# Preparing the cross-attention inside the last self-attention group of a decoder layer

## The chip, the cores and the metric

One Trainium2 chip, one core. The metric is the device time of one execution in microseconds (us); the kernel before has a median of 1537.75 us over three runs.

## The reference

One pre-norm decoder layer over x of 8 sequences x 256 tokens x 1024 channels, in float32. Each of its three parts normalises x (mean and variance over the channels) and adds its result to x:

- Self-attention with 32 query and 8 key/value heads of 32 channels. The four projections have weights of sign(w) only and a scale per output channel.
- Cross-attention with 16 heads of 64: `C_q = norm(x) @ Wq_d` (1024 to 128), `C_kv = ctx @ Wkv_d` (1024 to 64), `CqWqk = C_q @ W_qk` (128 to 1024), scores = CqWqk . C_kv / 8 per head, softmax, values = `C_kv @ Wv_u`.
- A gated feed-forward part through rank 256, inner width 2752.

## The kernel before

**Tiling.** The 2048 tokens are worked in four groups of 512 (two sequences, four row tiles of 128). Before a projection each normalised row tile is transposed by PE in two halves (step `turn`, four 128x128 transposes into one bank of PSUM) and evacuated as two parts whose sum is the float32 value (step `split`: ACT writes the high part, L993, DVE subtracts for the low part, L1201). All products with float32 operands are three or two such passes.

**One order for all engines.** A list `ORDER` of steps (`self_order`, L100; `cross_order`, L236; `ffn_order`) is walked by all five engine programs, and each does its share of every step. So the place of a step in the list sets its place in each engine's queue and in SP's queue of DMA issues; an engine that waits in one step does nothing behind it. Two PSUM banks (`proj`) serve all turns and projections in turn; `bank_uses` hands them out in list order.

**Self-attention of a group.** It has 64 head steps (8 key/value heads x 2 sequences x 4 heads). Head i does: `tile` (scores on PE L778, exp on ACT L1017, and on every second head a fold, the sum of two tiles of exps, on POOL L1465), `score` of head i+16 (PE L758, DVE maximum L1270), and, every fourth head, `mix` (values, PE L791) and `sums` (PE L804), after which `sum_turn`, `recip_turn` (DVE) and `finish` (POOL L1483, L1488, L1491, which writes attnT_hi and attnT_lo) normalise a unit of 8 heads. ACT copies the mixed values (L1023) only after POOL's L1483 of the unit before. The exps live in eight `wide` buffers, the folds in four. The rest of each head step is a plan `side[i]`: in groups 0 to 2 the loads, norms and turns of the next group's x (turns at heads 34 to 41) and its first q projections (heads 43 to 63). In the last group the plan is empty from head 34 on. `late` holds the six steps that follow head 63: finish of unit 6; sums and mix; sums; sum_turn; recip_turn; finish of unit 7.

**The seam.** After `late` the last group's output projection runs (`o`, PE L863: 8 tiles x 16 matmuls; DVE L1319 and L1323 add the residual; SP stores x1). `("phase", 2)` then makes ACT, DVE, POOL and SP wait until all self-attention results are made, since the cross-attention's buffers lie over the self-attention's. `cross_order` begins: turns of y (norm of x1) and c (ctx, not normalised) tiles, four each; the raw weights loaded into `x_group` memory (SP L1621 to L1625), high parts made by POOL (L1499 to L1511), low parts by DVE (L1330 to L1343); `lowq` (C_q, PE L877), eight loads of x1 into `x_group` (SP L1630), two `xq` (PE L887; ACT, DVE; eight stack copies by SP L1640), `lowkv` (C_kv, PE L877), loads of group 1's first three row tiles, five `vup` (PE L897), and then the heads of cross-attention: `score` (PE L821, DVE L1298, exps on ACT L1034), flip, evac, values. `attention_order` starts with three scores and then a lead: the norm of y tile 0 of group 1, then v-ups 5 to 7. The first turn of that y tile comes in the first head.

**Row tiles.** Loads go through two rings of row buffers, `xin` (3) and `xres` (2). A load waits on SP until the step that last used its buffer is done (`released`, L607); for a row tile that is the PE transpose of its second half.

## Time and profile before

| | |
|---|---|
| median of three runs | 1537.75 us (1535.91 to 1538.12) |
| the profiled execution | 1539.78 us |
| its span, first to last instruction | 1538.0 us |
| mean granted clock of TensorE | 0.973 |
| PE, DVE, ACT, POOL busy | 91%, 59%, 46%, 34% |
| self-attention heads, groups 0 to 3 | about 77 to 605 us |
| last o projection | 614 to 644.5 us |
| first cross-attention scores | 693.9 us |

An engine's row in the timeline gives the start, the length, the line, what it writes and reads, and in brackets how long the engine stood idle before it and what released it. Lengths of matmuls overlap, since they are pipelined; the distance of two starts is the rate.

### The profile page before, as it was taken

What the parts mean: (1) busy time and instruction counts of PE and PEld (TensorE: products, weight loads), DVE (VectorE), ACT (ScalarE), POOL (GpSimd) and SP (SyncE); (2) the same over time, 40 slices, a digit from 0 to 9 for tenths busy, and PEclk for the clock granted to TensorE, in tenths of its full rate; (3) what the DMA queues carried; (4) which work ended last, traced back from release to release, by engine and by line L of the source; (5) the groups of instructions that cost most, each with busy time, mean ns of one, the idle gap of its engine ahead of it and who ended that gap; (6) DMA issues with size and microseconds to landing.
All of it is one profiled execution on the core that took longest, in us unless ns stands there. A gap on an engine that the chain in (4) does not pass through costs nothing.

```text
span 1538.0 us, 22614 instructions
## 1 busy us (share of the span) xinstructions
PE 1393.0 (91%) x8423; PEld 981.8 (64%) x8423; DVE 908.7 (59%) x1611; ACT 704.8 (46%) x1584; POOL 523.7 (34%) x466
## 2 busy tenths in 40 slices
PE   5888899999999996868989899896999999999998
PEld 3555455555555553447667677675788888887886
DVE  5468555836774563547658486473563663673645
ACT  5165503541452254026747476472553354454452
POOL 2047503851674168112112121031442342342320
PEclk9999899999999998979999999997999999999999
DMA  5776634574537351455536445257210310310111
GB/s 192 104 141 129 118 69 125 92 115 106 108 60 118 105 82 44 147 152 141 164 96 166 137 111 137 70 151 259 76 57 0 110 56 1 110 55 1 69 69 55
DMA packets 94881, 157.55 MB, mean 102 GB/s; under 512 B 9910, under 2 KB 49076, under 8 KB 94772
## 3 DMA queue, kind: packets, MB, share of 16 engines
q1 hardware_dynamic: 94772, 156.11, 41.0%
q8 instruction: 67, 1.10, 0.3%
q14 instruction: 42, 0.34, 0.1%
HBM read 82.15 MB, written 25.17 MB: 70 GB/s over the span
## 4 chain that ended last, share of the span: by engine, by line
PE 66%; DMA 10%; DVE 9%; ACT 5%; issue 4%; SPq 3%; POOL 3%; DVEq 0%; POOLq 0%; ACTq 0%
PE bank L937 15%; PE bank L949 7%; PE bank L863 7%; DMA q_stack<-hi_lo 6%; PE bank L744 5%; PE bank L922 3%; PE bank L698 3%; PE bank L877 3%; PE bank L778 3%; PE bank L758 3%; PE bank L791 2%; PE bank L821 2%; PE bank L848 2%; PE bank L962 2%; DMA xq_stack<-xhi_lo 2%
## 5 line engine op out<-in xcount | busy, mean ns | idle before, releaser
L1465 POOL TENSOR_TENSOR fold<-wide 128x512 f32<-128x512 f32 x128 | 163.2, 1286 | 238.7 <-ACT wide L1017 222.1
L1017 ACT ACTIVATE wide<-bank 128x512 f32<-128x512 f32 x256 | 150.0, 596 | 144.0 <-PE bank L778 141.4
L1270 DVE TENSOR_REDUCE neg_top<-bank 128x2 f32<-128x512 f32 x256 | 170.6, 680 | 61.2 <-PE bank L758 59.7
L1541 POOL TENSOR_TENSOR v_lo<-v_all,v_hi 128x512 fp32r<-128x512 f32 x88 | 122.7, 1396 | 246.5 <-ACT v_hi L1102 246.5
L778 PE MATMUL bank<-q_stack,k_stack 98*128 98x512 f32 x256 | 138.7, 545 | 4.0 <-ACT wide L1017 3.7
L937 PE MATMUL bank<-pT_hi,v_hi 128*128 128x512 f32 x352 | 137.3, 390 | 2.6 <-POOL v_lo L1541 2.6
L937 PE MATMUL bank<-pT_hi,v_lo 128*128 128x512 f32 x352 | 137.2, 390 | 0.0
L937 PE MATMUL bank<-pT_lo,v_hi 128*128 128x512 f32 x352 | 136.9, 389 | 0.0
L1422 DVE SCALAR_TENSOR_TENSOR inner<-bank,b_cols,inner 128x512 f32<-128x512 f32 x88 | 65.9, 749 | 112.6 <-PE bank L937 109.3
L758 PE MATMUL bank<-k_stack,q_stack 96*128 96x256 f32 x512 | 111.6, 305 | 16.1 <-DMA q_stack<-hi_lo 13.9
L1034 ACT ACTIVATE wide<-bank,neg_max 128x256 f32<-128x256 f32 x256 | 120.2, 489 | 10.0 <-DVE neg_max L1298 10.0
L758 PEld LDWEIGHTS bank<-k_stack,q_stack 96*128 96x128 f32 x512 | 93.9, 195 | 43.2 <-DMA q_stack<-hi_lo 19.7
L1125 ACT ACTIVATE inner_hl<-inner 128x512 fp32r<-128x512 f32 x88 | 55.6, 632 | 135.4 <-DVE inner L1422 135.4
L949 PE MATMUL bank<-inner_hl,u_hi 128*128 128x512 f32 x352 | 111.3, 397 | 3.7 <-DVE inner_hl L1425 3.7
L1298 DVE TENSOR_REDUCE neg_max<-bank 128x2 f32<-128x512 f32 x128 | 87.1, 685 | 41.0 <-PE bank L821 40.7
L1518 POOL TENSOR_TENSOR x_group<-x_group,tmp 128x512 f32<-128x512 f32 x32 | 40.9, 1278 | 198.4 <-DVE tmp L1382 198.4
L863 PE MATMUL bank<-signs_o,attnT_hi 128*128 128x512 f16 x256 | 99.2, 387 | 8.6 <-POOL attnT_lo L1491 8.0
L1473 POOL TENSOR_TENSOR bn<-bn,neg_half 128x1 f32<-128x1 f32 x48 | 29.9, 622 | 222.3 <-DVE bn L1195 222.3
L744 PE MATMUL bank<-hT_hi,signs_qkv 128*128 128x512 f16 x256 | 100.3, 392 | 1.5 <-DVE hi_lo L1246 1.5
L1425 DVE TENSOR_TENSOR inner_hl<-inner,inner_hl 128x512 fp32r<-128x512 f32 x88 | 65.0, 738 | 61.5 <-ACT inner_hl L1125 61.5
L698 PE MATMUL bank<-ident,xin 128*128 128x128 f32 x456 | 74.7, 293 | 29.3 <-DVE hT_lo L1201 9.3
L863 PE MATMUL bank<-signs_o,attnT_lo 128*128 128x512 f16 x256 | 98.7, 386 | 0.0
(176 smaller groups left out, 3136.5 us busy)
## 6 DMA issues: line engine op xcount, KB each, us to landing
q_stack<-hi_lo SPq DMA_DIRECT2D x96, 256.0 KB, 5.7
xin<-x_scratch SPq DMA_DIRECT2D x33, 512.0 KB, 4.7
xq_stack<-xhi_lo SPq DMA_DIRECT2D x128, 128.0 KB, 2.4
x_res<-in_x SPq DMA_DIRECT2D x22, 512.0 KB, 4.7
x_scratch<-x_res SPq DMA_DIRECT2D x16, 512.0 KB, 2.8
xin<-in_ctx SPq DMA_DIRECT2D x16, 512.0 KB, 4.6
x_group<-x_scratch SPq DMA_DIRECT2D x32, 256.0 KB, 3.3
x_scratch<-x_group SPq DMA_DIRECT2D x32, 256.0 KB, 2.6
```

The lines of the kernel that those rows point to most:

```text
L698: t = pe.transpose(J[:, i * P:(i + 1) * P], src[:, kb * P:(kb + 1) * P], ident[:, :])
L744: t = pe.matmul(J[:, :], sW[:, kb, tq * P:(tq + 1) * P], hT[p][:, kb, :], start=kb == 0 and p == 0, stop=kb == KB - 1 and p == 1)
L758: t = pe.matmul(tops[n % 2][:, a * SEQ:(a + 1) * SEQ], qst[U % Q_STACKS][0:SUB, r, b * SEQ + a * P:b * SEQ + (a + 1) * P], kst[0:SUB, tq, ...
L778: pe.matmul(tiles[m % 2][:, :], kst[0:SUB + 2, tq, b * SEQ + kt * P:b * SEQ + (kt + 1) * P], qst[U % Q_STACKS][0:SUB + 2, 2 * hp:2 * hp + ...
L863: t = pe.matmul(J[:, :], OT[p][:, tq, m * P:(m + 1) * P], sWo[:, tq, n * GT:(n + 1) * GT], start=tq == 0 and p == 0, stop=tq == KB - 1 and ...
L937: t = pe.matmul(G[:, :], v1s[W % 3][wp][:, s, r, :], pT[g % 2][ap][:, r, :], start=r == 0 and (wp, ap) == (0, 0), stop=r == RB - 1 and wp ...
L949: t = pe.matmul(z_banks[r][:, :], u2s[W % 3][wp][:, r, :], inner_hl[W % 2][:, ap, :], start=f == 0 and (wp, ap) == (0, 0), stop=f == FB - ...
L1017: act.activation(PT[m % PT_RING][:, :], tiles[m % 2][:, :], ACT.Exp).then_inc(sem["tile_exped"], 1)
L1034: t = act.activation(Pb[:, a * SEQ:(a + 1) * SEQ], S[:, a * SEQ:(a + 1) * SEQ], ACT.Exp, bias=mx[:, a:a + 1], accum_out=total)
L1270: dve.tensor_reduce(neg_top[U % 2][:, r, b, :], tops[n % 2][:, :].rearrange("p (a b) -> p a b", a=QT), AX.X, ALU.max, negate=True).then_in ...
L1465: pool.tensor_tensor(fold[f % FOLD_RING][:, :], PT[2 * f % PT_RING][:, :], PT[(2 * f + 1) % PT_RING][:, :], ALU.add).then_inc(sem["folded" ...
L1541: pool.tensor_tensor(lo[:, :, :, 0:n], inner_gu(f, n), hi[:, :, :, 0:n].bitcast(F32), ALU.subtract).then_inc(sem["iw_lo"], 1)
```

## The change

Names: y is the normalised x1, c the context; raw weights are numbered 0 (Wq_d), 1 (Wkv_d), 2 (W_qk), 3 (Wv_u).

- The last group's plan gets the load and split of raw weight 1, loads, turns and splits of all c and y tiles of cross-attention group 0, the four y norms, `lowkv` in eight chunks of three matmuls (heads 46 to 53), and the loads of raw weights 0, 2 and 3 (heads 58, 60, 62).
- Behind head 63, `raw_split` 0, the first half of the first o tile and `lowq` stand between the late steps; `raw_split` 2 and 3 and the first two `xq` stand in the o projection.
- Raw weights land in the row rings, not in `x_group`; their high parts are made by ACT in place of POOL. DVE still makes the low parts.
- Memory is laid out anew: `ckv0`, `actT1` (c) and `wkv_down` over the signs and hT of the q/k/v projections, `actT0` (y) over `hi_lo` and three of four query stacks, `wq_down` over the fourth, `w_qk`, `ckv1` and `wv_up` over the key stack. Waits guard this: c splits and raw_split 1 wait for the last q projection, y splits for all stack copies and the tiles up to head 55, the other raw splits for all tiles, the first evacuation of `lowq` for all sums.
- The o matmuls wait for attnT_lo of four units per half, not for all eight at once.
- `cross_order` starts with the `x_group` loads and the three loads of group 1, then five `vup`.

```diff
-        put(57, ("o_load", g, 1))
+        if g + 1 < NG:
+            put(57, ("o_load", g, 1))
+        else:
+
+            put(7, ("raw_load", 1))
+            for m, at in enumerate((12, 16, 20, 36)):
+                put(at, ("load", "c", 0, m))
+            put(34, ("raw_split", 1))
+            for m, at in enumerate((34, 36, 38, 42)):
+                for h in range(2):
+                    put(at + h, *turn("c", 0, m, h))
+            for m, at in enumerate((38, 40, 44, 45)):
+                put(at, ("load", "y", 0, m))
+                put(at + 6, ("norm", "y", 0, m))
+            for c in range(KB):
+                put(46 + c, ("lowkv", 0, c))
+            put(46 + KB - 1, ("lowkv_out", 0))
+            for m in range(TILES):
+                for h in range(2):
+                    put(56 + 2 * m + h, *turn("y", 0, m, h))
+            for i, at in ((0, 58), (2, 60), (3, 62)):
+                put(at, ("raw_load", i))
...
-            for step in late:
-                order += step
-            for i in range(2 * TILES):
+            order += late[0] + late[1] + [("raw_split", 0), ("o_load", g, 1)] + o_parts(g, 0)[0]
+            order += late[2] + late[3] + late[4] + [("lowq", 0), ("lowq_out", 0), ("raw_split", 2)] + late[5]
+            order += o_parts(g, 0)[1]
+            for i in range(1, 2 * TILES):
                 for part in o_parts(g, i):
                     order += part
                 if i in (1, 3):
                     order.append(("o_load", g, i // 2 + 2))
-                if i < 3:
-                    order.append(("load", "y", 0, i))
-                elif i < 6:
-                    order.append(("norm", "y", 0, i - 3))
+                if i == 2:
+                    order.append(("raw_split", 3))
+                if i in (3, 4):
+                    order += [("xq", 0, i - 3), ("xq_out", 0, i - 3)]
...
-    order = []
-    for i, t in enumerate((0, 1, 2, 4, 5, 3, 6, 7)):
-        order += turn(0, t, 0) + turn(0, t, 1)
-        if i < 5:
-            order.append(load(0, i + 3))
-        if i == 2:
-            order += [("raw_load",), ("norm", "y", 0, 3)]
-        if i >= 4:
-            order.append(("raw_split", i - 4))
-        if i == 6:
-            order += whole("lowq", 0)
-    order += [("xg_load", 0, j) for j in range(XPAIRS)]
+    low_kv = lambda g: [("lowkv", g, c) for c in range(KB)] + [("lowkv_out", g)]
+    order = [("xg_load", 0, j) for j in range(XPAIRS)]
     late = []
     for g in range(NG):
         if g:
-            order += whole("lowq", g)
-        order += late + whole("xq", g, 0) + whole("xq", g, 1) + whole("lowkv", g)
-        if g == 0:
+            order += whole("lowq", g) + late + whole("xq", g, 0) + whole("xq", g, 1) + low_kv(g)
...
+        else:
             order += [load(1, t) for t in range(3)]
...
-CHUNKED = ("q", "o", "down")
+CHUNKED = ("q", "o", "down", "lowkv")
...
-            ring = "xres" if (ph == "x" and (m == 3 or g == 0 and m != 2)) or (ph, g, m) == ("z", 0, 3) else "xin"
-        elif step[0] == "wload" or step == ("u1_load", 1):
+            ring = "xres" if (ph == "x" and (m == 3 or g == 0 and m != 2)) or (ph, g, m) in (("y", 0, 3), ("z", 0, 3)) else "xin"
+        elif step[0] == "wload" or step == ("u1_load", 1) or step[0] == "raw_load" and step[1] != 1:
             ring = "xin"
-        elif step[0] in ("o_load", "v2_load") or step == ("u1_load", 0):
+        elif step[0] in ("o_load", "v2_load") or step in (("u1_load", 0), ("raw_load", 1)):
...
-    actT = {ph: [sb(f"actT_hi{i}", [P, KB, GT], F32R, mem), sb(f"actT_lo{i}", [P, KB, GT], F32R, mem)]
-            for i, ph in enumerate("yc")}
-    wqd = [sb(f"wq_down_{n}", [P, KB, LQ], F32R, mem) for n in ("hi", "lo")]
-    wqk = [sb(f"w_qk_{n}", [P, XH * XD], F32R, mem) for n in ("hi", "lo")]
-    wkv = [sb(f"wkv_down_{n}", [P, KB, 2, XD], F32R, mem) for n in ("hi", "lo")]
+    hi_lo = lambda name, shape: [sb(f"{name}_{n}", shape, F32R, mem) for n in ("hi", "lo")]
+    ckv = [sb("ckv0", [P, 2, GT], F32R, mem)]
+    actT = {"c": hi_lo("actT1", [P, KB, GT])}
+    wkv = hi_lo("wkv_down", [P, KB, 2, XD])
+    actT["y"] = hi_lo("actT0", [P, KB, GT])
+    wqd = hi_lo("wq_down", [P, KB, LQ])
+    wqk = hi_lo("w_qk", [P, XH * XD])
+    ckv.append(sb("ckv1", [P, 2, GT], F32R, mem))
     wvu = sb("wv_up", [P, XH * XD], F32R, mem)
     cq = sb("cq_hi_lo", [P, 2, GT], F32R, mem)
...
+        if load[0] == "raw_load":
+            return sem["raw_lo"], RAW_SPLIT[load[1]]
         if load[0] == "v2_load":
             return sem["v2_lo"], load[1] + 1
         return stored[ROWS[load][1]], 16 * STORES[load]
 
+    def self_rows_used(e):
+
+        _, full, use = bank_of("q_out", NG - 1, KV_HEADS - 1)
+        e.wait_ge(full, use + 1)
+
+    def query_stacks_used(e):
+
+        uses = NG * (KT + KB) // 2
+        for b in range(2):
+            e.wait_ge(stacked[b], 48 * uses)
+        e.wait_ge(sem["tiled"], SELF_HEADS - UH)
...
+        if ph == "c" and g == 0:
+            self_rows_used(e)
+        if ph == "y" and g == 0:
+            query_stacks_used(e)
...
-                    e.wait_ge(sem["attn_lo"], KV_HEADS * (g + 1))
                     bank_free(e, "o_out", g, i)
+                e.wait_ge(sem["attn_lo"], KV_HEADS * g + 4 * (c + 1))
...
+            elif kind == "lowkv":
+                g, kb = at
+                J, full, use = bank_of("lowkv_out", g)
+                if kb == 0:
+                    group_turned(e, "c", g)
+                    e.wait_ge(sem["raw_lo"], RAW_SPLIT[1])
+                    bank_free(e, "lowkv_out", g)
+                for wp, ap in PASSES:
+                    t = pe.matmul(J[:, :], wkv[wp][:, kb, :, :].rearrange("p c n -> p (c n)"), actT["c"][ap][:, kb, :],
+                                  start=kb == 0 and (wp, ap) == (0, 0), stop=kb == KB - 1 and wp == 1)
+                if kb == KB - 1:
+                    t.then_inc(full, 1)
...
+            elif kind == "raw_split":
+                i = at[0]
+                buf, land, count = row_of("raw_load", i)
+                e.wait_ge(land, count)
+                if i == 1:
+                    self_rows_used(e)
+                    for c in range(2):
+                        act.activation(wkv[0][:, :, c, :], buf[:, 0:KB * XD].rearrange("p (k n) -> p k n", k=KB),
+                                       ACT.Copy).then_inc(sem["raw_hi"], 1)
+                else:
+                    if i == 3:
+                        e.wait_ge(sem["raw_vu"], 16)
+                    e.wait_ge(sem["tiled"], SELF_HEADS)
+                    hi = wqd[0][:, :, :].rearrange("p k n -> p (k n)") if i == 0 else wqk[0][:, :] if i == 2 else wvu[:, :]
+                    act.activation(hi, buf[:, :], ACT.Copy).then_inc(sem["raw_hi"], 1)
...
+                    if g == 0:
+                        e.wait_ge(sem["summed"], GB * SELF_UNITS)
...
-                    pool.tensor_scalar(wqd[0][:, :, :], raw_qd, 1.0, 0.0, ALU.mult, ALU.add).then_inc(sem["raw_hi"], 1)
...
+                step = (kind, i)
+                buf, land, count = row_of(*step)
+                if ROWS_BEFORE[step]:
+                    e.wait_ge(*released(ROWS_BEFORE[step]))
+                if i == 0:
+                    sp.dma_start(buf[:, :].rearrange("p (k n) -> p k n", k=KB),
+                                 wq_d.rearrange("(k p) n -> p k n", p=P)).then_inc(land, 16)
+                elif i == 1:
+                    sp.dma_start(buf[:, 0:KB * XD].rearrange("p (k n) -> p k n", k=KB),
+                                 wkv_d.rearrange("(k p) n -> p k n", p=P)).then_inc(land, 16)
+                elif i == 2:
+                    sp.dma_start(buf[:, :], w_qk).then_inc(land, 16)
+                else:
+                    sp.dma_start(buf[0:XD, :], wv_u).then_inc(land, 16)
+                    sp.dma_start(buf[XD:P, :], wv_u).then_inc(sem["raw_vu"], 16)
...
-                e.wait_ge(sem["raw_lo"], 5)
                 x1_ready(e, g)
```

## Rows read from the trace of the kernel before

**Rows 1.** The page: span, and its first section, busy us of TensorE.
```profile
span 1538.0 us, 22614 instructions
...
PE 1393.0 (91%) x8423; PEld 981.8 (64%) x8423; DVE 908.7 (59%) x1611; ACT 704.8 (46%) x1584; POOL 523.7 (34%) x466
```

**Rows 2.** Timeline of PE: tile matmuls of heads 34, 44, 63, groups 2 and 3.
```profile
431.38 0.50 PE L778 MATMUL bank<-q_stack,k_stack 98*128 98x512 f32 x1
...
448.03 0.59 PE L778 MATMUL bank<-q_stack,k_stack 98*128 98x512 f32 x1
...
471.14 0.59 PE L778 MATMUL bank<-q_stack,k_stack 98*128 98x512 f32 x1
...
571.02 0.50 PE L778 MATMUL bank<-q_stack,k_stack 98*128 98x512 f32 x1
...
584.21 0.50 PE L778 MATMUL bank<-q_stack,k_stack 98*128 98x512 f32 x1
...
604.16 1.22 PE L778 MATMUL bank<-q_stack,k_stack 98*128 98x512 f32 x2
```

**Rows 3.** Stretches: length, PE, PEld, DVE, ACT, POOL busy, PE clock, DMA share, GB/s.
```profile
135.90:180.10 44.20, 41.25 (x350) 23.79 (x346) 28.14 (x58) 33.05 (x60) 30.19 (x27) 0.96 0.62 126
431.30:471.10 39.80, 37.24 (x308) 20.90 (x305) 23.11 (x43) 24.10 (x45) 30.23 (x27) 1.00 0.48 74
571.10:604.80 33.70, 27.57 (x228) 14.97 (x228) 15.87 (x29) 17.82 (x34) 27.82 (x25) 0.92 0.30 72
...
434.00:446.00 12.00, 9.48 (x88) 6.34 (x88) 11.30 (x23) 7.07 (x14) 7.96 (x8) 1.00 0.37 45
```

**Rows 4.** Timeline of PE from the last sums to the first turn of group 1.
```profile
607.49 0.64 PE L804 MATMUL bank<-fold,ones 128*32 128x256 f32 x8 [0.25 <-POOL fold L1465]
614.03 0.61 PE L863 MATMUL bank<-signs_o,attnT_hi 128*128 128x512 f16 x1 [5.90 <-POOL attnT_lo L1491]
...
619.93 0.38 PE L863 MATMUL bank<-signs_o,attnT_hi 128*128 128x512 f16 x1
...
644.32 0.38 PE L863 MATMUL bank<-signs_o,attnT_lo 128*128 128x512 f16 x1
...
653.44 1.48 PE L698 MATMUL bank<-ident,xin 128*128 128x128 f32 x8 [2.27 <-DMA xin<-in_ctx]
...
680.59 0.50 PE L877 MATMUL bank<-actT_hi,wkv_down_hi 128*128 128x512 f32 x1 [1.01 <-DVE xhi_lo L1357]
...
687.75 1.19 PE L897 MATMUL bank<-wv_up,ckv 128*128 128x512 f32 x4 [1.41 <-DVE ckv L1350]
...
693.90 2.08 PE L821 MATMUL bank<-ckv,xq_stack 128*128 128x256 f32 x12 [2.38 <-DMA xq_stack<-xhi_lo]
...
701.84 1.11 PE L698 MATMUL bank<-ident,xin 128*128 128x128 f32 x4 [2.29 <-POOL xin L1475]
```

**Rows 5.** Timeline of ACT, SP's DMA issues and DVE over the same stretch.
```profile
608.75 0.60 ACT L1023 ACTIVATE attnT_raw<-bank 128x512 f32<-128x512 f32 x1 [2.67 <-POOL attnT L1483]
...
679.84 5.28 SPq L1630 DMA_DIRECT2D x_group<-x_scratch  x8
...
691.15 1.54 SPq L1568 DMA_DIRECT2D xin<-x_scratch  x3
...
698.07 1.28 DVE L1189 BATCH_NORM_STATS2 bn<-xin 128x6 f32<-128x512 f32 x2 [1.36 <-DMA xin<-x_scratch]
```

**Rows 6.** Single operations: DVE's timeline, groups of POOL, and the page's loads.
```profile
660.79 1.63 DVE L1330 TENSOR_TENSOR wq_down_lo<-x_group,wq_down_hi 128x1024 fp32r<-128x1024 f32 x1
...
668.62 1.21 DVE L1339 TENSOR_TENSOR w_qk_lo<-x_group,w_qk_hi 128x1024 fp32r<-128x1024 f32 x1
...
L1473 POOL TENSOR_TENSOR bn<-bn,neg_half 128x1 f32<-128x1 f32 x48 | 29.9, 622 | 222.3 <-DVE bn L1195 222.3
L1475 POOL TENSOR_SCALAR xin<-xin,bn 128x1024 f32<-128x1024 f32 x41 | 50.5, 1231 | 4.3
...
xin<-x_scratch SPq DMA_DIRECT2D x33, 512.0 KB, 4.7
```

More of the change, by code:

```diff
@@ L463, in build_program @@
     mem = ExitStack()
+    sg = [sb(f"sign{i}", [P, D], F16, mem) for i in range(2)]
     sW = sb("signs_qkv", [P, KB, D + 2 * KVD], F16, mem)
+    hT = [sb("hT_hi", [P, KB, GT], F16, mem), sb("hT_lo", [P, KB, GT], F16, mem)]
+    hl = [sb(f"hi_lo{i}", [P, 2, GT], F32R, mem) for i in range(2)]
+    qst = [sb(f"q_stack{i}", [P, REP, GT], F32R, mem) for i in range(Q_STACKS)]
+    kst = sb("k_stack", [P, KV_HEADS, GT], F32R, mem)
+    fold = [sb(f"fold{i}", [P, GT], F32, mem) for i in range(FOLD_RING)]
+    vall = sb("v_all", [P, TILES, KVD], F32, mem)
+    sum_cols = sb("sum_cols", [P, GT], F32, mem)
+    R_sb = sb("recip_rows", [P, GT], F32, mem)
+    OTs_self = sb("attnT_raw", [P, GT], F32, mem)
+    OTn = sb("attnT", [P, GT], F32, mem)
     sWo = sb("signs_o", [P, KB, D], F16, mem)
+    OT = [sb("attnT_hi", [P, KB, GT], F16, mem), sb("attnT_lo", [P, KB, GT], F16, mem)]
+    recip = sb("recip_cols", [P, GT // 32], F32, mem)
     sc_rows = sb("scale_rows", [NSC, P], F32, mem)
@@ L473, in build_program @@
     v_most = sb("v_most", [P, 2], F32, mem)
-    sg = [sb(f"sign{i}", [P, D], F16, mem) for i in range(2)]
-    hT = [sb("hT_hi", [P, KB, GT], F16, mem), sb("hT_lo", [P, KB, GT], F16, mem)]
-    kst = sb("k_stack", [P, KV_HEADS, GT], F32R, mem)
-    vall = sb("v_all", [P, TILES, KVD], F32, mem)
-    hl = [sb(f"hi_lo{i}", [P, 2, GT], F32R, mem) for i in range(2)]
-    qst = [sb(f"q_stack{i}", [P, REP, GT], F32R, mem) for i in range(Q_STACKS)]
-    OT = [sb("attnT_hi", [P, KB, GT], F16, mem), sb("attnT_lo", [P, KB, GT], F16, mem)]
     neg_top = [sb(f"neg_top{i}", [P, REP, GB, QT], F32, mem) for i in range(2)]
     top_rows = [sb(f"top_rows{i}", [REP * GB * QT, 2, P], F32R, mem) for i in range(2)]
-    fold = [sb(f"fold{i}", [P, GT], F32, mem) for i in range(FOLD_RING)]
-    sum_cols = sb("sum_cols", [P, GT], F32, mem)
-    recip = sb("recip_cols", [P, GT // 32], F32, mem)
-    R_sb = sb("recip_rows", [P, GT], F32, mem)
-    OTs_self = sb("attnT_raw", [P, GT], F32, mem)
-    OTn = sb("attnT", [P, GT], F32, mem)
     mem.close()
@@ L866, in tensor_program @@
                     t.then_inc(full, 1)
[L867 removed]
+            elif kind == "lowq":
                 g = at[0]
[L869 to L873 removed]
+                J, full, use = bank_of("lowq_out", g)
+                group_turned(e, "y", g)
+                e.wait_ge(sem["raw_lo"], RAW_SPLIT[0])
+                bank_free(e, "lowq_out", g)
                 for kb in range(KB):
                     for wp, ap in PASSES:
[L876 to L878 removed]
+                        t = pe.matmul(J[:, :], wqd[wp][:, kb, :], actT["y"][ap][:, kb, :],
+                                      start=kb == 0 and (wp, ap) == (0, 0), stop=kb == KB - 1 and wp == 1)
                 t.then_inc(full, 1)
+            elif kind == "lowkv":
[7 more added lines that the diff above has]
+                    t = pe.matmul(J[:, :], wkv[wp][:, kb, :, :].rearrange("p c n -> p (c n)"), actT["c"][ap][:, kb, :],
+                                  start=kb == 0 and (wp, ap) == (0, 0), stop=kb == KB - 1 and wp == 1)
+                if kb == KB - 1:
+                    t.then_inc(full, 1)
             elif kind == "xq":
@@ L1055, in scalar_program @@
                 else:
+                    if g == 0:
+                        e.wait_ge(sem["sign_set"], NSC)
                     if g > 1:
```

76 lines of the change are left out of this document (26 added, 50 removed).

## The prediction, made before the changed kernel ran

> **What bounds it now.** I read the page first: TensorE (PE) is busy 91% of the span [rows 1], so time is to be had only where PE stands idle or runs at the lower clock. Next came the stretches: the slices of ten microseconds put the thinnest ones between the last self-attention head and the first cross-attention scores. The timeline of PE there [rows 4] is the basis of the forecast. The last tile of self-attention starts at 604.77 (the second of the x2 row) [rows 2]. PE then waits 5.90 us for the last attnT_lo; the first o matmuls run at 0.421 us apiece until 619.93 and at 0.216 after that (113 steps from 619.93 to 644.32), so 14 of them lose 2.9 us to the 1.2 GHz level. From 644.5 to 668 PE transposes eight row tiles of y and c with one slot free at a time. Three times it waits 2 to 3 us for c rows; the row at 653.44 is one of them. The q-down projection, kv-down (680.59) and v-up (687.75) follow in series, and the first score comes at 693.90, or 89.1 us after the last tile. The o projection at full rate would need 128 x 0.216 = 27.6 of those.
>
> **The cover.** The change puts kv-down and all 16 half-tile turns beside heads 34 to 63 of the last group. The best gauge is the same place one group earlier. There, heads 34 to 63 carry 8 turns and 48 q matmuls and take 471.14 - 431.38 = 39.76 us; the last group, with neither, takes 604.77 - 571.02 = 33.75 [rows 2]. Side work of some 15 us of PE thus costs 6.0 there. Heads 0 to 33 gain only four or five loads; group 2 has such loads and takes 0.4 us longer there, which I charge.
>
> **Heads 34 to 44.** Group 2 takes 448.03 - 431.38 = 16.65, the last group 584.21 - 571.02 = 13.19 [rows 2]. With eight turns of c in place of eight of x, that is +3.5. In that stretch DVE, not PE, is full: 11.30 of 12 us [rows 3]. So the two subtractions of raw_split 1, which the change puts there, are not hidden: +1.5 (two of 0.68 us each, from 1.4 to 3.0). ACT's two copies for it lie in ACT's free time (7.07 of 12 busy).
>
> The range of that term comes from a row: w_qk_lo took 1.21 us and wq_down_lo, the same shape, 1.63, with POOL at work beside it [rows 6]. The Trainium skill (SBUF — State Buffer, "Who interferes with whom" and "two separate sides") says that a VectorE operation with two SBUF inputs and a GpSimd one that reads SBUF shut each other out for a whole instruction. By that rule each of the five subtractions, now beside folds and finishes, could wait out a POOL operation: some 3 us on the path where I have 1.9. The trace agrees in direction (0.42 us).
>
> **Heads 44 to 63.** Group 2: 471.14 - 448.03 = 23.1; the last: 20.6. The PE work that comes in is 24 kv-down matmuls (from 680.59 to the first v-up, 7.16 us less the 1.41 waited: 5.75 with the drain, 5.5 taken) and seven half turns at 0.6, together 9.7, about what group 2 has (46 q matmuls of 0.216 = 9.9). But it is bunched. Group 2 needs 1.22 us a head with 0.5 of side work, so 0.72 without; eight heads with 0.69 of kv-down take 1.4 each, seven with a turn 1.4 (ACT has exp, split and a share of a copy, about 1.3), and four bare ones 1.08: 25.3, or +4.7. POOL gets four norms in eight heads: 4 x (0.62 + 1.23) = 7.4 us [rows 6] on top of 27.8 busy in 33.7 [rows 3], which fits in some 43 us; the burst itself falls into 11 us of heads, where POOL's idle share of 5.9 in 33.7 leaves 1.9, so it is 5.5 late, inside the ring of eight wide buffers (eight heads). I charge nothing for it and keep it for a rival. The heads cost 0.4 + 3.5 + 1.5 + 4.7 = **+10.1**; bounds +6.0 (group 2 as a whole) and +14 (group 0, with signs besides, takes 44.2 [rows 3], +10.5, and 3.5 for the burst).
>
> **SP.** The new loads wait in SP's order for slots: c tile 3 (head 36) for the turn at 35, y tiles for the turns at 37, 39 and 43, the raw weights for turns at 57 to 61. Behind them are the top rows of heads 41 and 49, needed at 48 and 56. Each wait is one or two heads, each load has six heads, some 8 us, to land: nothing charged.
>
> **The tail**, on the clock of the old trace. One half turn comes after the last tile: +0.7. ACT can copy attnT_raw only when POOL's multiply of the unit before allows it (608.75 [rows 5]), so at 609.4, and only then comes raw_split 0: two widths of 0.6 less one overhead, 1.05, ending at 611.1; DVE's subtraction, 1.2 to 1.6, ends at 612.5. q-down waits for it. PE has 8 o matmuls (1.7) and the last sums before it, so it idles some 2 us where it idled 5.90. Behind the subtraction on DVE stands the last sum_turn, and the last attnT_lo moves from 614.0 to about 617; q-down covers that. q-down: 5.5, and +1.3 for the lower clock (0 to 2.9, from the o matmuls of before): 619.3. Then 120 o matmuls, 25.9; six of xq with two short bank waits, 2.3: 647.5. Five v-ups, 3.8 (6.15 less 2.38, rounded [rows 4]): the first score at 651.3, **42.6 earlier**.
>
> **What is late next.** The eight xq stack copies and their 2.38 us wait [rows 4] are long done. After phase 2, SP issues eight x_group loads (5.28 us) and only then the rows of group 1; before, these waits were hidden behind kv-down. DVE ends the last o_out about 1.5 after the last o matmul: 649.0; loads at 654.3. The old trace goes from the first x_group issue to the norm's start in 18.2 us (679.84 to 698.07 [rows 5]) and moves 3.67 MB in it (eight x_group loads, eight stack copies, a row tile). Without the stack copies 2.62 MB are in front, 13 us: 662.0. A landing of 6.9 us after its own issue (691.15 to 698.07) would give 661.2. The norm stands in DVE's order ahead of the v-up and probT copies, and PE's next turn waits for it, so everything resumes there: 698.07 - 661.8 = **36.3 earlier**, not 42.6. From there on the order is as before.
>
> **Sum:** -36.3 + 10.1 = -26.2 against the profiled execution's 1539.8: 1513.6. That execution lies 2.0 above the median of the three runs, so 1511.5 as a median.
>
> **Rivals.**
> - *The reload does not bind* (the loads are quick or DVE has other work): -42.6 + 10.1 gives 1505; with heads as cheap as group 2's, 1501. Against it: 2.62 MB cannot land much faster than the 18.2 us above show. Chance 0.17.
> - *POOL and DVE become the bound of the heads.* The norm burst holds folds, folds hold exps, and the turn of y waits; the last fold and both finishes come late. That is +14 instead of +10 and 3 to 5 more in the tail: 1516 to 1521. For it: POOL is already busy for 27.8 of 33.7 us there, and DVE for 11.3 of 12 at the turns [rows 3]. Chance 0.22.
> - *The work goes nowhere*: the guards of the overlaid memory (stacks used, all tiles done) hold the y turns until the heads end. Then some 10 us of turns and copies return to the tail: 1522. Against it: the guard asks for head 55, the first y turn stands at 56. Chance 0.02.
> - *Slower.* Loads in three slots become round trips inside the heads: if the turn of c tile 3 and each y norm find their rows not landed, every one of the five loads stops PE's order, and with it the exps, for a load (4.7 [rows 6]) and a norm (3.8, from 698.07 to 701.84 [rows 4, 5]): 42 us lost where 36 are won, and the heads' own 10: 1554. It decides if a load takes longer than its six heads, 8 us. The median landing of such a load is 4.7. Chance 0.03, and 0.02 for something between that nets nothing.
>
> **The numbers.** My forecast, 1506 to 1516, has 0.54; the two neighbours reach to 1501 and 1522. What can be told from no change is 0.2%, 3 us. Faster 0.95, same 0.02, slower 0.03. Range 1501 to 1522.
>
> **What would show it.** Heads 34 to 63 of the last group at about 43.5 us, the 34 to 44 part near 18; DVE over 90% busy there. Between the last tile and q-down, about 8 us, with PE's longest wait on wq_down_lo. The first score some 46.5 us after the last tile instead of 89.1. After it a wait of PE and DVE for the rows of group 1, 5 to 8 us long. Wrong if heads 34 to 63 take under 40 or over 48, or if no wait for xin stands after the first scores.

## The result and the profile after

The changed kernel takes **1522.06 us** (median of five runs, 1520.06 to 1528.59). The kernel before stands at 1537.75 beside it, the ratio is 0.9905 [0.989, 0.992]. That is a gain of 15.7 us where 26 were forecast: the forecast's 1511.5 is 10.6 off, and the result lies 0.06 us above the upper end of the range, 1522. The profiled execution took 1523.0 us. Its page begins so (the columns are those of [rows 1]):

```profile
span 1521.2 us, 22619 instructions
...
PE 1383.8 (91%) x8423; PEld 979.3 (64%) x8423; DVE 906.7 (60%) x1611; ACT 707.1 (46%) x1589; POOL 517.7 (34%) x461
```

The span is 16.8 shorter. Where it went is read from PE's timeline of the changed kernel: the tile matmuls of heads 34, 44 and 63 of the last group, and then the first work after them.

```profile
575.49 0.50 PE L808 MATMUL bank<-q_stack,k_stack 98*128 98x512 f32 x1
...
590.84 0.48 PE L808 MATMUL bank<-q_stack,k_stack 98*128 98x512 f32 x1
...
615.84 0.50 PE L808 MATMUL bank<-q_stack,k_stack 98*128 98x512 f32 x1 [2.42 <-ACT wide L1062]
...
621.87 0.48 PE L808 MATMUL bank<-q_stack,k_stack 98*128 98x512 f32 x1
...
624.29 0.64 PE L834 MATMUL bank<-fold,ones 128*32 128x256 f32 x8 [1.50 <-DVE sum_cols L1350]
...
630.10 0.56 PE L910 MATMUL bank<-actT_hi,wq_down_hi 128*128 128x512 f32 x1 [1.91 <-DVE wq_down_lo L1408]
...
669.75 1.58 PE L856 MATMUL bank<-ckv,xq_stack 128*128 128x256 f32 x12
...
683.71 1.12 PE L728 MATMUL bank<-ident,xin 128*128 128x128 f32 x4 [9.24 <-POOL xin L1539]
```

| stretch | before | after | difference | forecast |
|---|---|---|---|---|
| start to head 0 of the last group | 511.8 | 514.5 | +2.7 | 0 |
| its heads 0 to 34 | 59.26 | 60.94 | +1.7 | +0.4 |
| heads 34 to 44 | 13.19 | 15.35 | +2.2 | +5.0 |
| heads 44 to 63 | 20.56 | 31.03 | +10.5 | +4.7 |
| last tile to group 1's first turn | 97.07 | 61.84 | -35.2 | -36.3 |
| the rest | 836.2 | 837.5 | +1.3 | 0 |

The seam came nearly as forecast: q-down starts 8.2 us after the last tile (about 8 forecast), the first score 47.9 after it (46.5 forecast), and then PE stands 9.24 us for the rows of group 1 (5 to 8 forecast). Of the 9.4 us that are missing, 7.0 were lost in front of the last tile: up to there the kernel is 17.1 us later, where 10.1 were forecast.

The last wait's cause, on SP and DVE:

```profile
667.19 6.03 SPq L1687 DMA_DIRECT2D x_group<-x_scratch  x8
...
673.26 1.70 SPq L1615 DMA_DIRECT2D xin<-x_scratch  x3
...
679.86 1.29 DVE L1256 BATCH_NORM_STATS2 bn<-xin 128x6 f32<-128x512 f32 x2 [7.43 <-DMA xin<-x_scratch]
```

From the first x_group issue to the norm it takes 12.7 us (13 forecast; 18.2 before [rows 5]). The wait has an after-effect: PE's granted clock is at the 1.2 GHz level (0.50) from within the wait until some 4.5 us behind it (columns of [rows 3]).

```profile
678.20:688.20 10.00, 4.49 (x18) 4.20 (x19) 6.32 (x15) 1.63 (x5) 3.49 (x4) 0.50 0.24 95
```

The stretches of the changed kernel, in the same columns: heads 34 to 63, then heads 34 to 44 and 44 to 63 alone, and the part in which the norms of y meet the folds.

```profile
575.50:621.90 46.40, 37.82 (x316) 25.42 (x312) 31.25 (x63) 26.83 (x52) 35.38 (x33) 0.96 0.43 114
575.50:590.80 15.30, 12.36 (x114) 9.40 (x111) 12.37 (x22) 10.37 (x21) 8.19 (x8) 1.00 0.71 157
590.80:621.90 31.10, 25.46 (x204) 16.03 (x202) 18.88 (x41) 16.46 (x32) 27.19 (x26) 0.95 0.29 94
590.80:602.00 11.20, 9.33 (x78) 5.61 (x76) 10.53 (x24) 4.99 (x10) 9.45 (x10) 1.00 0.27 96
602.00:612.00 10.00, 9.46 (x81) 5.96 (x78) 5.39 (x14) 6.55 (x12) 9.62 (x10) 1.00 0.18 61
595.50:619.00 23.50, 18.36 (x136) 11.87 (x135) 13.37 (x31) 12.43 (x25) 22.72 (x22) 0.95 0.22 68
```

For 23.5 us POOL is the full engine, with 22.72 busy, and PE is not, with 18.36. How POOL reaches PE is to be seen in the timelines of POOL and ACT. The multiply that reads attnT_raw (L1547) comes out of POOL's order late, behind norms and folds. ACT's copy into attnT_raw (L1068), which needs that buffer free, waits for it, and the exps stand in ACT's order behind the copy, so PE's tile at 615.84 above waits 2.42 us for the bank that an exp has yet to read.

```profile
598.52 0.55 POOL L1537 TENSOR_TENSOR bn<-bn,neg_half 128x1 f32<-128x1 f32 x1
599.18 1.19 POOL L1539 TENSOR_SCALAR xin<-xin,bn 128x1024 f32<-128x1024 f32 x1
600.34 1.28 POOL L1529 TENSOR_TENSOR fold<-wide 128x512 f32<-128x512 f32 x1
601.58 1.28 POOL L1547 TENSOR_TENSOR attnT<-attnT_raw,recip_rows 128x512 f32<-128x512 f32 x1
...
613.35 1.26 POOL L1547 TENSOR_TENSOR attnT<-attnT_raw,recip_rows 128x512 f32<-128x512 f32 x1
```

```profile
602.95 0.60 ACT L1068 ACTIVATE attnT_raw<-bank 128x512 f32<-128x512 f32 x1 [2.61 <-POOL attnT L1547]
603.45 1.78 ACT L1062 ACTIVATE wide<-bank 128x512 f32<-128x512 f32 x3
...
614.71 0.60 ACT L1068 ACTIVATE attnT_raw<-bank 128x512 f32<-128x512 f32 x1 [3.23 <-POOL attnT L1547]
```

ACT's waits in heads 34 to 63, summed (us in total, times, longest), are 7.5 us for this one cause. In the kernel before they are 3.2 (its row is the last). No wait of ACT for a fold is among them.

```profile
ACT wide L1062 <- PE bank L808: 8.1, 9, 1.8
ACT attnT_raw L1068 <- POOL attnT L1547: 7.5, 3, 3.2
...
ACT attnT_raw L1023 <- POOL attnT L1483: 3.2, 2, 1.8
```

More goes with PE's wait than its 2.42 us: right behind it the granted clock falls to the 1.2 GHz level (0.50) for 3.4 us:

```profile
616.70:620.10 3.40, 2.95 (x17) 2.21 (x21) 1.68 (x3) 2.69 (x6) 2.32 (x2) 0.50 0.00 0
```

One caution for what follows: with the heads' code unchanged, heads 34 to 63 of the last group take 46.4 us in this trace, but 49.25 in the trace of the earlier reload, 49.45 in that of the padding and 49.06 in that of the exchanged blocks. The granted clock differs between them. The reload's trace has 0.90 in heads 34 to 44 and 0.90 behind them, where this trace has 1.00 and 0.95:

```profile
577.15:593.80 16.65, 13.71 (x114) 10.28 (x111) 12.48 (x22) 10.34 (x21) 8.22 (x8) 0.90 0.65 144
593.80:626.40 32.60, 26.89 (x203) 16.54 (x202) 18.90 (x41) 16.62 (x32) 27.30 (x26) 0.90 0.33 98
```

So the trace in the table above is the shortest of the four, and the other three pass the 48 us that the prediction names as a sign of being wrong. A difference of less than 3 us in one stretch of one trace proves nothing unless the clocks in it agree; the timed ratios decide.

### The profile page after: what moved, and what is told of

Same layout as the page of the kernel before. It is cut to its first block, busy times and chain, and to the rows that moved or that the text cites. A ratio compares the mean times of both kernels' runs of the same rounds, so it can differ in the third digit from the quotient of the medians.

```text
span 1521.2 us, 22619 instructions
## 1 busy us (share of the span) xinstructions
PE 1383.8 (91%) x8423; PEld 979.3 (64%) x8423; DVE 906.7 (60%) x1611; ACT 707.1 (46%) x1589; POOL 517.7 (34%) x461
## 4 chain that ended last, share of the span: by engine, by line
PE 66%; DMA 10%; DVE 10%; ACT 5%; issue 4%; SPq 3%; POOL 2%; DVEq 0%; POOLq 0%; ACTq 0%
PE bank L982 15%; PE bank L994 7%; PE bank L898 7%; DMA q_stack<-hi_lo 6%; PE bank L774 5%; PE bank L967 3%; PE bank L808 3%; PE bank L728 3%; PE bank L788 3%; PE bank L856 2%; PE bank L821 2%; PE bank L883 2%; PE bank L1007 2%; DMA xq_stack<-xhi_lo 2%; PE bank L868 2%
## 5 line engine op out<-in xcount | busy, mean ns | idle before, releaser
L788 PEld LDWEIGHTS bank<-k_stack,q_stack 96*128 96x128 f32 x512 | 94.7, 196 | 47.9 <-DMA q_stack<-hi_lo 21.3
L1188 ACT ACTIVATE inner<-bank,b_cols 128x512 f32<-128x512 f32 x88 | 60.5, 687 | 82.7 <-PE bank L982 82.6
L774 PE MATMUL bank<-hT_lo,signs_qkv 128*128 128x512 f16 x256 | 98.6, 385 | 0.0
```

Of the source, the lines that this page charges most:

```text
L774: t = pe.matmul(J[:, :], sW[:, kb, tq * P:(tq + 1) * P], hT[p][:, kb, :], start=kb == 0 and p == 0, stop=kb == KB - 1 and p == 1)
L788: t = pe.matmul(tops[n % 2][:, a * SEQ:(a + 1) * SEQ], qst[U % Q_STACKS][0:SUB, r, b * SEQ + a * P:b * SEQ + (a + 1) * P], kst[0:SUB, tq, ...
```

## The experiments

Ratios are to the kernel before, timed beside each kernel on the same chip; the changed kernel's own is 0.9905 [0.989, 0.992]. The experiments ran on three chips, so ratios are compared here, not times. The theory: 10 us are missing, a part for memory placement, a part for POOL's late multiply through ACT; and a further 8 us could be had from the reload, which binds as forecast. The rivals: the placement costs nothing and the loads in the heads do it; POOL's own load, not the copy's buffer, sets the heads.

### The layout alone

The kernel before with the changed kernel's memory layout (both lists of buffers in the new order) and nothing else: the same steps, the same waits.

```diff
     mem = ExitStack()
+    sg = [sb(f"sign{i}", [P, D], F16, mem) for i in range(2)]
     sW = sb("signs_qkv", [P, KB, D + 2 * KVD], F16, mem)
+    hT = [sb("hT_hi", [P, KB, GT], F16, mem), sb("hT_lo", [P, KB, GT], F16, mem)]
+    hl = [sb(f"hi_lo{i}", [P, 2, GT], F32R, mem) for i in range(2)]
+    qst = [sb(f"q_stack{i}", [P, REP, GT], F32R, mem) for i in range(Q_STACKS)]
+    kst = sb("k_stack", [P, KV_HEADS, GT], F32R, mem)
+    fold = [sb(f"fold{i}", [P, GT], F32, mem) for i in range(FOLD_RING)]
...
```

> The kernel before in its own order, with only the new memory layout of the self-attention and cross-attention buffers. Before the changed kernel reaches a single moved step it is already late: its first head starts at 79.6 us instead of 77.5, heads 0 to 33 of groups 1 and 2 take 0.9 and 0.6 us longer each, and the last group's head 0 comes 2.7 us later. Theory A (placement): the stack copies and loads run slower at the new addresses; then this kernel shows the same late head 0 of the last group (514.5 instead of 511.8) and is 2.5 to 4 us slower than the kernel before. Theory B (variation from one execution to the next): it is within 1 us of the kernel before and its head 0 of the last group lies where chance puts it.

1543.72 us, ratio 1.0034 [1.0017, 1.0051]: 5.2 us slower, from addresses alone, and a little more than the 2.5 to 4 expected. The last group's head 0 starts at 518.4 in its trace, not at the 514.5 expected. The trace shows where it starts to differ. The copies of hi_lo into the query stacks land later (the page's DMA issues: count, KB, median us from issue to landing), and PE waits for them longer (total, times, longest), 17.7 us where the kernel before has 13.9. This kernel's rows, then those of the kernel before:

```profile
q_stack<-hi_lo SPq DMA_DIRECT2D x96, 256.0 KB, 6.0
PE bank L760 <- DMA q_stack<-hi_lo: 17.7, 14, 4.7
...
q_stack<-hi_lo SPq DMA_DIRECT2D x96, 256.0 KB, 5.7
PE bank L758 <- DMA q_stack<-hi_lo: 13.9, 13, 4.6
```

Two halves of the layout, on the kernel before. First hi_lo, the query stacks and the key stack at the front of the self-attention's memory, all else in its old order; then the new order of all else, but those three left at about their old place (by the lists, hi_lo and the query stacks exactly there, the key stack 4 KB further on). The first one's edit:

```diff
     mem = ExitStack()
+    hl = [sb(f"hi_lo{i}", [P, 2, GT], F32R, mem) for i in range(2)]
+    qst = [sb(f"q_stack{i}", [P, REP, GT], F32R, mem) for i in range(Q_STACKS)]
+    kst = sb("k_stack", [P, KV_HEADS, GT], F32R, mem)
     sW = sb("signs_qkv", [P, KB, D + 2 * KVD], F16, mem)
...
```

> The kernel before with only hi_lo, the query stacks and the key stack moved to the front of the self-attention memory; everything else keeps its sequence. The whole new layout cost 0.34%, with the last tile at 612.9 us against 604.8 and 606.9 in the two traces with the old one. Theory (where the stacks lie decides): most of it is seen here, a ratio of 1.002 to 1.005 and the last tile at 609 to 613. Rival (it is another buffer, such as the operands of the q matmuls): ratio within 0.15% of 1, last tile at 604 to 607.

> The counterpart of the run before: the kernel before with the new layout, but key stack, hi_lo and query stacks left at about their old place (71 to 127 thousand bytes into the memory). Theory (where the stacks lie decides): ratio within 0.15% of 1, last tile at 604 to 607. Rival (another buffer): 1.002 to 1.005, last tile at 609 to 613.

Stacks in front: 1541.84, ratio 1.0034 [1.0021, 1.0047]. All else new: 1536.49, ratio 0.9987 [0.997, 1.0004]. The whole cost goes with the three. The page of the second has the old landing time:

```profile
q_stack<-hi_lo SPq DMA_DIRECT2D x96, 256.0 KB, 5.6
```

Is it the low bits of the address? The changed kernel with 2376 bytes per partition ahead of both lists, which gives the stacks their old offsets modulo 4096:

```diff
     mem = ExitStack()
+    sb("pad_self", [P, 594], F32, mem)
     sg = [sb(f"sign{i}", [P, D], F16, mem) for i in range(2)]
...
     mem = ExitStack()
+    sb("pad_cross", [P, 594], F32, mem)
...
```

> The changed kernel with 2376 unused bytes in each partition ahead of both overlaid memories, so that hi_lo, the query stacks and the key stack have the same offsets modulo 4096 as in the kernel before; order and overlay are unchanged. The layout alone cost 0.34% (0.17 to 0.51) when put into the kernel before, with the stack copies landing after a median of 6.0 us instead of 5.7 and PE waiting 17.7 us for them instead of 13.9. Theory A (low address bits): the copies land as before and the kernel is 3 to 5 us faster than the changed one, about 1518. Theory B (the absolute place, or the neighbourhood of hi_lo and the stacks, decides): no change beyond 1.5 us, the copies still land after 5.9 to 6.0.

1524.19, ratio 0.9917 [0.9898, 0.9936]: no gain, landing 5.9. Then the same question at large: the changed kernel with the two blocks of the overlaid memory exchanged, so that the stacks lie far back again (by the lists, 18 KB behind their old place).

```diff
     mem = ExitStack()
-    sg = [sb(f"sign{i}", [P, D], F16, mem) for i in range(2)]
...
-    kst = sb("k_stack", [P, KV_HEADS, GT], F32R, mem)
     fold = [sb(f"fold{i}", [P, GT], F32, mem) for i in range(FOLD_RING)]
...
     top_rows = [sb(f"top_rows{i}", [REP * GB * QT, 2, P], F32R, mem) for i in range(2)]
+    sg = [sb(f"sign{i}", [P, D], F16, mem) for i in range(2)]
...
+    kst = sb("k_stack", [P, KV_HEADS, GT], F32R, mem)
...
```

> The changed kernel with the two blocks of the overlaid memory exchanged (folds, sums, output signs and attnT first; signs, hT, hi_lo, stacks behind them), so that the stacks lie far back again, with the same sharing and the same order of work. If the place of the stacks costs the changed kernel what it cost the kernel before (0.34%, 5 us): ratio to the kernel before 0.987, some 5 us under the changed kernel, the copies of the query stacks landing in 5.6 or 5.7 us instead of 5.9, and PE's waits for them 13 to 14.5 us instead of 15.8. If the 0.34% is tied to another property of that layout, or is not felt in the changed kernel: 0.990 to 0.992 as before.

1525.72, ratio 0.9913 [0.9898, 0.9928]. The placement branch of the expectation missed. The stacks lie far back, and the copies still land in 6.0 us, with 17.4 us of waits. So "in front" is not the property that goes with slow copies:

```profile
q_stack<-hi_lo SPq DMA_DIRECT2D x96, 256.0 KB, 6.0
```

Last, on the kernel before, the copies' source alone: hi_lo stands at the front, and what lay ahead of it moves 8 KB back, the key stack too. The query stacks stay exactly where they were (the text on record has them 8 KB further on, which holds for the key stack alone).

```diff
     mem = ExitStack()
+    hl = [sb(f"hi_lo{i}", [P, 2, GT], F32R, mem) for i in range(2)]
     sW = sb("signs_qkv", [P, KB, D + 2 * KVD], F16, mem)
...
-    hl = [sb(f"hi_lo{i}", [P, 2, GT], F32R, mem) for i in range(2)]
```

> The kernel before with hi_lo alone (the source of the stack copies) moved to the front of the self-attention's memory; stacks and k stack stay back, 8 KB further on. If the source's place decides the landing time: 5.9 us, waits 16, ratio 1.0034. If the destination's place does: 5.6 to 5.7, waits 13 to 14.5, ratio 1.000.

1539.15, ratio 1.0003 [0.999, 1.0017]; landing 5.8, waits 14.5. The source's place alone costs no time. The clearest sign in the traces is the sum of heads 0 to 34 over groups 1 to 3, where the stacks are filled: 178.4 us before, 178.9 with all else new, 179.0 with hi_lo moved; 181.1 with the whole layout, 180.1 with the stacks in front, 181.5 in the changed kernel, 181.7 padded, 182.6 exchanged (in these three the last group's share holds the added loads too). The kernels fall into two kinds, and the changed kernel is of the costly one in every layout that was tried. Without the last group the split is as clear: 118.9 to 119.4 us for heads 0 to 34 of groups 1 and 2 in the four traces of one kind, the second buffer on the kernel before (below) among them, and 120.0 to 121.6 in the traces named here of the other. Which property of the place decides it stays open. By the lists of buffers, two properties divide the kinds, and no run here separates them: in every cheap layout the query stacks keep their old address and the key stack lies ahead of them, and in every costly one they have a new address and the key stack lies right behind them.

### The reload

Group 1's three row loads go out during the o projection instead of behind the eight x_group loads.

```diff
                 if i in (3, 4):
                     order += [("xq", 0, i - 3), ("xq_out", 0, i - 3)]
+                if i in (4, 5, 6):
+                    order.append(("load", "y", 1, i - 4))
...
-        else:
-            order += [load(1, t) for t in range(3)]
...
```

> The changed kernel, with the loads of the first three y row tiles of group 1 issued in the o projection (after o tiles 4, 5 and 6) instead of behind the eight x_group loads. Theory of the prediction (the reload is what binds after the first scores): the 9.24 us wait of PE before the first turn of group 1 goes to under 2.5 us and the kernel is 7 to 9 us faster than the changed one, about 1514. Rival (the norm and turn only hide the next bound, for instance the xq stack copies): under 3 us.

1514.35, ratio 0.9843 [0.9824, 0.9863]: 0.62% or 9.5 us under the changed kernel. SP's queue and PE's first turn of group 1 in its trace:

```profile
663.04 0.59 SPq L1615 DMA_DIRECT2D xin<-x_scratch  x1
...
664.16 1.71 SPq L1615 DMA_DIRECT2D xin<-x_scratch  x2
...
670.06 6.65 SPq L1687 DMA_DIRECT2D x_group<-x_scratch  x8
```

```profile
672.62 1.59 PE L856 MATMUL bank<-ckv,xq_stack 128*128 128x256 f32 x12
...
679.07 0.66 PE L728 MATMUL bank<-ident,xin 128*128 128x128 f32 x4 [1.72 <-POOL xin L1539]
```

From the first score to that turn it is 6.5 us instead of 14.0; the wait of 9.24 is 1.72. The stretch at the 1.2 GHz level that came with the long wait is gone too: what follows the turn takes 834.1 us instead of 837.5. The forecast's "what is late next" is shown.

### The norms and the copy

The y norms at heads 44, 48, 52 and 56 instead of 44, 46, 50 and 51:

```diff
-                put(at + 6, ("norm", "y", 0, m))
+                put((44, 48, 52, 56)[m], ("norm", "y", 0, m))
```

> The changed kernel, with the four y norms at heads 44, 48, 52 and 56 instead of 44, 46, 50 and 51; the amount of work is unchanged. Theory (burst): POOL, busy without a gap from 595.4 to 619.0, is late because the norms are bunched, folds and ACT's copies of the mixed values wait for it; spread out, heads 34 to 63 of the last group take 42 to 44 us instead of 46.4, and the kernel is 2 to 4 us faster. Rival 1 (total): POOL's total of folds, finishes and norms is the bound; spreading gives under 1 us. Rival 2: the last norm at head 56 makes the last y turns late; 0 to 2 us slower.

1523.19, ratio 0.9901 [0.9885, 0.9916]: the same. ACT waits 8.3 us for POOL's multiply, no less than the 7.5 of the changed kernel. The burst as such is not what costs here.

A second attnT_raw buffer, so that ACT's copy waits for the multiply of two units before:

```diff
-                if U:
-                    e.wait_ge(sem["attn_out"], U)
-                act.activation(OTs_self[:, :], mixed[:, :], ACT.Copy).then_inc(sem["mix_copied"], 1)
+                if U > 1:
+                    e.wait_ge(sem["attn_out"], U - 1)
+                act.activation(OTs_self[U % 2][:, :], mixed[:, :], ACT.Copy).then_inc(sem["mix_copied"], 1)
...
```

> The changed kernel with a second attnT_raw buffer, so that ACT's copy of the mixed values no longer waits for POOL's multiply of the unit before it (waits of 2.61, 3.23 and 3.25 us between head 50 and the tail), and with it the exps and splits queued behind that copy. Theory (ACT stands behind a late POOL): heads 34 to 63 of the last group get 3 to 6 us shorter and wq_down_hi in the tail comes 2 to 3 us earlier: 4 to 8 us faster in all. Rival (POOL itself is the bound, ACT's waits are only its shadow): the folds hold the exps instead, under 2 us.

1517.75, ratio 0.986 [0.9841, 0.9878]: 0.45% or 6.9 us under the changed kernel. Heads 34 to 63 take 43.35, and the gain lies in heads 44 to 63: 26.6 us, at a granted clock of 1.00. The five traces with one buffer and all the norms on POOL have 31.0 to 32.7 there, so this difference is beyond the caution above. In the tail q-down starts 7.0 us after the last tile instead of 8.2. ACT's copies in those heads wait for PE now and for POOL no more (the stretch of heads 44 to 63, then ACT's timeline):

```profile
594.40:621.10 26.70, 23.68 (x204) 15.14 (x202) 18.89 (x41) 16.09 (x31) 24.79 (x25) 1.00 0.35 106
```

```profile
605.44 0.60 ACT L1069 ACTIVATE attnT_raw<-bank 128x512 f32<-128x512 f32 x1 [1.89 <-PE bank L822]
...
615.00 0.60 ACT L1069 ACTIVATE attnT_raw<-bank 128x512 f32<-128x512 f32 x1 [0.48 <-PE bank L822]
```

The same edit on the kernel before, to see whether the wait was costly there already:

> The kernel before, in its old order and layout, with only the second attnT_raw buffer. It tells whether ACT's wait for POOL's multiply is a cost that the change made (it has 7.5 us of such waits in heads 34 to 63 of the last group where the kernel before has 3.2) or one that was there. Theory (made by the change, since exps had slack before): under 2 us faster, the 2.7 us before the last copy being hidden behind POOL's own chain. Rival: as much as in the changed kernel, 4 to 6 us.

1538.11, ratio 0.9998 [0.9983, 1.0013]: nothing that shows, and 2.6 us at most. The wait became costly through what the change puts beside these heads; that POOL's norms are the part that matters is what the next kernel's trace shows.

How much of it is POOL's row-wide work itself? In the next kernel POOL's norm multiply of the four y tiles covers one column of 1024, so that the first 512 tokens of y go into the cross-attention unnormalised; the rest is as in the changed kernel.

```diff
-                pool.tensor_scalar(buf[:, :], buf[:, :], st[:, 12:13], st[:, 15:16], ALU.add, ALU.mult).then_inc(
+                n = 1 if at[:2] == ["y", 0] else D
+                pool.tensor_scalar(buf[:, 0:n], buf[:, 0:n], st[:, 12:13], st[:, 15:16], ALU.add, ALU.mult).then_inc(
...
```

> The changed kernel, with POOL's multiply of the four y norms of group 0 cut down to one column (it leaves out the normalisation of the first 512 tokens for the cross-attention; the four powers stay). That takes 4 times 1.2 us off POOL between heads 44 and 56 and nothing off PE, ACT or DVE. Theory (POOL's total is the bound there): heads 34 to 63 of the last group, 46 to 49 us in the kernels so far, take 42 to 44, and the kernel is 3 to 6 us faster. Rival (the turns, splits and maxima on PE, ACT and DVE are the bound, POOL only looks full): under 1.5 us.

1520.03, ratio 0.9885 [0.9864, 0.9905]; heads 34 to 63 43.89, of which heads 44 to 63 are 27.2 at a clock of 1.00, ACT's wait for the multiply 2.3. In the trace it gives nearly what the second buffer gives. In time its interval touches the changed kernel's, so that the ratio settles nothing for it alone.

The multiply on DVE instead:

```diff
+                if at[:2] == ["y", 0]:
+                    e.wait_ge(sem["ln_pow"], k + 1)
+                    dve.tensor_scalar(buf[:, :], buf[:, :], st[:, 12:13], st[:, 15:16], ALU.add, ALU.mult).then_inc(
+                        sem["ln_done"], 1)
...
```

> The changed kernel with the large multiply of the four y norms of group 0 on DVE instead of POOL (four times 1.19 us off POOL; the power stays on POOL, so DVE waits for it behind POOL's folds). After the spread norms gained nothing, theory (POOL's total between heads 44 and 63 is the bound): heads 34 to 63 get 3 to 5 us shorter, the kernel 3 to 5 us faster, about 1518. Rival (DVE in its order now waits for POOL's power, and delays maxima and sum_turn): no gain, or up to 3 us slower.

1526.97, ratio 0.9939 [0.9916, 0.9962]: slower by 0.34%, though the intervals still touch. Heads 44 to 63 take 34.4. DVE now waits for POOL's power (L1541), with head maxima and splits queued behind it (DVE's waits in heads 34 to 63 and just behind them):

```profile
DVE xin L1265 <- POOL bn L1541: 4.3, 3, 3.0
```

### Together

> The changed kernel with both gains at once: the group 1 loads in the o projection (alone: ratio to the kernel before 0.984 against 0.990) and the second attnT_raw buffer (alone: 0.986). If they remove different waits, as the theory has it (one lies before the last head and in the tail, the other after the first scores), they add: 0.984 - 0.0045 = 0.980, about 1508. If both only uncover one common bound: 0.983 or more.

Reload and second buffer: 1507.86, ratio 0.9811 [0.9791, 0.983]. The two gains, 0.62% and 0.45%, add up to 0.9798, which lies in the interval; one common bound, 0.983 or more by the expectation, would be at its very edge. They are separate.

> The kernel with both gains (ratio 0.981), with the y norms spread over heads 44, 48, 52 and 56. In the changed kernel the spread gained nothing, with ACT standing behind POOL's finishes either way. Theory (with the second attnT_raw buffer ACT no longer does, so POOL may be late in bursts): spreading gains 1 to 2 us here. Rival (POOL's total stays the bound): within 1 us, and the last y turn may come late.

With the norms spread as well: 1504.46, ratio 0.9789 [0.9767, 0.9811], heads 34 to 63 40.46. It is the fastest kernel of this study, but the step over the one before (0.2%) is not shown, since the two intervals overlap. Of the 2.9 us by which its heads are shorter in the trace, 1.4 lie in heads 34 to 44, where its granted clock is 1.00 and that of the kernel before it 0.90.

> The best version so far (earlier reload, second attnT_raw buffer, norms spread; 0.979) with the two blocks exchanged in the same way. Placement theory: 0.9755, about 5 us less, 1499 to 1500. No placement cost: 0.979 again.

The same with the blocks exchanged: 1507.63, ratio 0.9808 [0.9788, 0.9829], landing 6.0. No gain from this place either, as in the pair above.

## Why the prediction was right in kind and wrong by ten

**The tail and what is late next: right.** -35.2 against -36.3. q-down, the first score and the first turn came within 1.5 us of their places, and the earlier reload shows the bound that was named: with that wait gone 9.5 us more are won. The rival in which the reload does not bind is excluded.

**Heads 34 to 44: too dear.** Forecast +5.0, measured +2.2. The step that failed is the transfer of group 2's pace to this stretch, with 1.5 more on top because DVE was taken as full there. DVE is busy for 12.37 of 15.30 us, 81%, where over 90% was forecast. No run took the two terms apart. Ten more traces have the same work in these heads: eight take 16.7 us at a mean clock of 0.90, which is +3.5, and two take 15.3 at 1.00. So +5.0 came in none, and the measured size hangs on the clock. Both subtractions of raw_split 1 took 1.29 us together, behind 0.81 us in which DVE stood.

By the Trainium skill (SBUF — State Buffer, "Who interferes with whom") such a subtraction and a POOL operation that reads SBUF exclude each other, and the lock is held for a whole instruction. The traces agree: the one that comes second is longer by what is left of the first, less 0.13 to 0.15 us. The fold that began at 578.80, 0.27 us before the second subtraction ended, took 1.40 instead of 1.28 us. In the kernel with the second buffer an attnT_lo on POOL began just after wq_down_lo on DVE, took 2.01 instead of 1.16 us, and ended 1.03 after it:

```profile
626.60 1.29 DVE L1409 TENSOR_TENSOR wq_down_lo<-xin,wq_down_hi 128x1024 fp32r<-128x1024 f32 x1 [1.83 <-ACT wq_down_hi L1106]
...
626.91 2.01 POOL L1556 TENSOR_TENSOR attnT_lo<-attnT,attnT_hi 128x512 f16<-128x512 f32 x1
```

In the changed kernel the overlaps were short, so the 3 us that the prediction named for this did not come.

**Heads 44 to 63: the step that failed.** The prediction says of POOL's norm burst that "it is 5.5 late, inside the ring of eight wide buffers (eight heads). I charge nothing for it". The ring is not the only thing that hangs on POOL. The finish steps stand in the same queue, attnT_raw has one buffer, and ACT's copy holds the exps. I had this very wait in the tail [rows 5] and did not look for it in the heads. +10.5 came instead of +4.7. The second buffer takes back 0.45%, and with it the stretch takes 26.6 us or +6.1, so the rest of the term was nearly right. The rival "POOL and DVE become the bound of the heads" was right in that POOL is the bound, and its +14 for the heads is near the +14.3 measured from head 0. That nearness is in part luck: the +14.3 holds 1.7 of heads 0 to 34, its route (folds hold exps) is not the one seen, DVE was not the bound, and its further 3 to 5 us in the tail did not come.

**The layout: a cost that had no line at all.** I priced every instruction that the change adds or moves, and took moved memory for free. On the kernel before, it costs 0.34% or 5.2 us. In the changed kernel the same signs stand (landing 5.9, heads 0 to 34 of groups 1 to 3 longer by 3.1 us); that it is the same 5 us there was not shown by a kernel that has it back, since neither other layout did. It is the likeliest account of 1.4 of the 2.7 us ahead of the last group (heads 0 to 34 of groups 1 and 2) and of most of the excess of 1.3 in its heads 0 to 34. The rest of the 2.7 stays open: in the four traces with the query stacks at their old place head 0 of the last group starts at 511.8, 513.0, 514.9 and 516.3, so the 514.5 of the changed kernel is no later than chance makes it, and the baseline of the table is the earliest of the four.

**Two slips in the rivals' sums** do not bear on the result: +14 with 3 to 5 us more in the tail is 1518 to 1521, not 1516 to 1521; and a c tile has no norm, so five round trips are 39 us, not 42.

**The sum.** Against the profiled execution: 2.7 before the last group, 1.3 in its heads 0 to 34, 3.0 in 34 to 63 (5.8 too little, 2.8 too much), 1.1 in the tail, 1.3 behind it: 9.4 of gain that did not come. The sign was right. What has to be explained is not the 0.06 us by which the range was missed, less than executions of one kernel differ, but the 9.4: the charge of nothing for POOL's lateness is its largest piece, and the too dear heads 34 to 44 hid half of that. The 1.3 behind the seam has no experiment of its own; the stretch at the 1.2 GHz level behind the long wait lies there.

## What to carry to other kernels

When work is moved onto an engine that looks idle, list every short step that the engine already does there, and for each the single buffer that it frees and the in-order engine that waits to refill it. A ring of eight gives no cover if another chain on the same engine has a ring of one. Look at the granted clock of a stretch before its length is compared between two traces. Price a new memory layout too: run the old kernel with the new layout alone before the change is judged.

## What was not expected of the hardware

The time of an SBUF-to-SBUF copy went with where its buffers lie. With the same 96 copies of 256 KB in the same order, the median from issue to landing was 5.6 to 5.7 us in one set of layouts and 5.9 to 6.0 in another. It was 5.8 with hi_lo alone moved, which cost no time, and the kernel before took 0.34% longer in two layouts of the second set. An offset of 2376 bytes did not change it, nor did the distance from the front alone. One kernel of the costly layout (the reload with the second buffer) shows a median of 5.7 and long heads 0 to 34 nevertheless, so the median is a sign and not a measure.
